# Attention on one core: bias tables loaded in quarters between transposing DMAs, and half of each head's share added by VectorE out of PSUM

## The reference

```python
qkv = (x @ qkv_w.T).reshape(Bb, Ss, 3, H, D)
...
scores = jnp.einsum('bhqd,bhkd->bhqk', q, k) * SCALE
...
dist = jnp.abs(pos[None, :] - pos[:, None])
kb = -p * jnp.log1p(a * dist)
attn = jax.nn.softmax(scores + kb[None], axis=-1)
out = jnp.einsum('bhqk,bhkd->bhqd', attn, v)
...
return out @ out_w.T
```

## Time and profile before

| | us |
|---|---|
| runs, median (lowest, highest) | 1968.41 (1962.46, 1969.35) |
| the profiled execution | 1962.84 |
| its span in the profile | 1961.1 |
| PE busy | 1809.5 |
| DVE busy | 1496.1 |
| ACT busy | 1163.7 |
| POOL busy | 1472.4 |

### The profile page before, as it was taken

One profiled execution on the slowest core, in us unless ns is written; L12 is line 12 of the kernel. 1 busy time (PEld: TensorE's weight loads), 2 busy tenths in 40 slices (PEclk: granted clock), 3 DMA queues, 4 the chain that ended last, 5 costly groups with the idle time before them and its releaser, 6 DMA issues. The chain is left out here.

```text
span 1961.1 us, 39818 instructions
## 1 busy us (share of the span) xinstructions
PE 1809.5 (92%) x12356; PEld 1048.2 (53%) x12356; DVE 1496.1 (76%) x2828; ACT 1163.7 (59%) x1724; POOL 1472.4 (75%) x871
## 2 busy tenths in 40 slices
PE   4999899998699999999999999999999999599988
PEld 3655633333355555555555555555555555256656
DVE  5244589999688788788788788788888788698841
ACT  6553422222677777777677777677777777322133
POOL 5250067778699899899899899899899899555421
PEclk8999999999799999999999999999999999799989
DMA  4254335464598988888888888888888988500001
GB/s 153 90 190 152 84 114 165 155 212 169 137 179 176 197 183 177 194 183 178 193 183 173 188 185 178 190 183 176 194 184 181 200 184 176 123 0 1 1 6 38
DMA packets 714150, 295.28 MB, mean 151 GB/s; under 512 B 619264, under 2 KB 678658, under 8 KB 714064
## 3 DMA queue, kind: packets, MB, share of 16 engines
q1 hardware_dynamic: 674784, 245.23, 56.8%
q10 hardware_dynamic: 37248, 46.14, 6.7%
q0 software_dynamic: 2048, 3.15, 0.6%
HBM read 102.39 MB, written 58.85 MB: 82 GB/s over the span
## 5 line engine op out<-in xcount | busy, mean ns | idle before, releaser
L1223 POOL TENSOR_TENSOR probs_lo<-probs 128x1024 bf16<-128x1024 f32 x512 | 958.1, 1900 | 80.4 <-DMA probs_t_lo<-probs_lo 54.4
L1191 ACT ACTIVATE probs<-scores,neg_max 128x1024 f32<-128x1024 f32 x512 | 588.7, 1150 | 266.2 <-DVE neg_max L1117 231.6
L1117 DVE CUSTOM_DVE_ANT_0 scores<-score_ps,bias_tab 128x1024 f32<-128x1024 f32 x512 | 624.9, 1221 | 120.1 <-issue 113.9
L1040 PE MATMUL score_ps<-k_hi_hi,q_hi_lo 128*128 128x512 bf16 x1024 | 392.8, 384 | 24.6 <-DVE ident_bf L1177 18.1
L1041 PE MATMUL score_ps<-k_lo_lo,q_hi_lo 128*128 128x512 bf16 x1024 | 391.1, 382 | 0.0
L1049 PEld LDWEIGHTS turn_ps<-ident_bf,probs 128*128 128x128 bf16 x4096 | 273.4, 99 | 146.7 <-issue 26.8
L1049 PE MATMUL turn_ps<-ident_bf,probs 128*128 128x128 bf16 x4096 | 316.0, 221 | 20.7 <-ACT probs L1191 20.7
L1068 PE MATMUL pv_ps<-probs_t_hi,v_hi_lo 128*128 128x512 bf16 x1024 | 262.9, 380 | 11.0 <-DVE share L1157 7.6
L1198 ACT COPY probs_t_hi<-turn_ps 128x1024 bf16<-128x1024 bf16 x256 | 255.8, 999 | 20.0 <-PE turn_ps L1049 16.1
L887 PE MATMUL proj_ps<-xn_t,wqk 128*128 128x512 f32 x512 | 232.7, 608 | 7.9 <-DVE rotated L777 5.9
L791 POOL TENSOR_TENSOR qk_parts<-rotated,qk_parts 128x1024 bf16<-128x1024 f32 x64 | 135.9, 2125 | 125.0 <-ACT qk_parts L785 124.7
(11 more groups left out here) (225 smaller groups left out, 2378.4 us busy)
## 6 DMA issues: line engine op xcount, KB each, us to landing
qk_parts<-qk_parts ACTq DMA_DIRECT2D x64, 512.0 KB, 3.4
q_hi_lo<-qk_parts SPq DMA_DIRECT2D x128, 128.0 KB, 2.8
k_hi_hi<-qk_parts SPq DMA_DIRECT2D x128, 128.0 KB, 2.9
k_lo_lo<-qk_parts SPq DMA_DIRECT2D x128, 128.0 KB, 2.9
v_hi_lo<-v_parts SPq DMA_DIRECT2D x64, 256.0 KB, 3.2
bias_tab<-bias_by_distance SPq DMA_DIRECT2D x16, 960.0 KB, 6.6
probs_t_lo<-probs_lo SPq DMA_TRANSPOSE x512, 3.3
v_parts<-cos_tables ACTq DMA_DIRECT2D x12, 512.0 KB, 2.7
```

The costliest lines, as they stand in the source:

```text
L1040: pe.matmul(o[:, cs[c]], QS[s][:, q], KS[s][:, cs[c]], start=True, stop=False)
L1117: v.tensor_tensor_reduce(SB[n % 2][:], sp_[n % 2][:], TB[s][:, j:j + S], -1.0, 3.0e38, ALU.add, ALU.min, neg_max[:, n % 16:n % 16 + 1]).th ...
L1191: act.activation(PR[n % NP][:], SB[n % 2][:], ACT.Exp, bias=neg_max[:, m:m + 1], scale=-1.0, accum_out=row_sum[:, m:m + 1]).then_inc(exped, 1)
L1223: g.tensor_tensor(LQ[n % NL][:], PR[n % NP][:], PRB[n % NP], ALU.subtract).then_inc(low_made, 1)
```

## The change

- `load_table` loads a quarter of a table (480 of 1920 columns, 240 KB).
- In `units`, the quarters of table s = 0 are issued behind `lo_turn` 9 to 12 of the group's last iteration; those of s = 1 behind `lo_turn` 0 to 3 of the next group's first iteration, so behind SP's branch back. A v load at n = 2 or 10 goes ahead of the quarter.
- `bias_max` waits on tile 0 for all four quarters.
- `scale_share` multiplies bank 0 as before. For bank 1 DVE runs four `scalar_tensor_tensor`, one for each row of `K.SACC`: PSUM times the row's scalar, plus the row. `SH` is one buffer, and POOL adds bank 0 alone, once a head.

```diff
@@ project, sync @@
-                load_table(sp, K, 0, s)
+                for k in range(4):
+                    load_table(sp, K, 0, s, k)
...
-def load_table(sp, K, g, s):
-
-    tab = bass.AP(tensor=K.fscr.tensor, offset=(g * 2 + s) * FLEN, ap=[[1, P], [1, TAB]])
-    sp.dma_start(K.TB[s][:], tab).then_inc(K.tab_in[s], DMA)
+def load_table(sp, K, g, s, k):
+
+    n = TAB // 4
+    tab = bass.AP(tensor=K.fscr.tensor, offset=(g * 2 + s) * FLEN + k * n, ap=[[1, P], [1, n]])
+    sp.dma_start(K.TB[s][:, k * n:k * n + n], tab).then_inc(K.tab_in[s], DMA)
...
-    SH = [sb(f"share{i}", [P, 4, D]) for i in range(2)]
+    SH = sb("share", [P, 4, D])
...
+        LOADS = (BT, U - 1)
...
-                    if n in (BT, U - 1) and not (last and b == B - 1):
-                        s = n // (U - 1)
+                    if n in LOADS and not (last and b == B - 1):
+                        s = LOADS.index(n)
...
                         load_scores_in(sp, K, it + 1, s)
-                        if b == B - 1:
-                            load_table(sp, K, g + 1, s)
+                    if LOADS[0] < n <= LOADS[0] + 4 and b == B - 1 and not last:
+                        load_table(sp, K, g + 1, 0, n - LOADS[0] - 1)
+                    k = (n - LOADS[1] - 1) % U
+                    if k < 4 and n > LOADS[1] and b == B - 1 and not last:
+                        load_table(sp, K, g + 1, 1, k)
+                    elif k < 4 and n < BT and b == 0 and not (isinstance(it, int) and it == 0):
+                        load_table(sp, K, g, 1, k)
...
-                    v.wait_ge(tab_in[s], (it + n // U) // B * DMA + DMA)
+                    v.wait_ge(tab_in[s], (it + n // U) // B * (4 * DMA) + 4 * DMA)
...
-                for c in range(2):
-                    v.wait_ge(op_ready, at(it, 4, 2 * hh + c + 1))
-                    v.wait_ge(added, at(it, 4, 2 * hh + c + 1))
-                    v.tensor_tensor(SH[c][:], ov[c][:], last_axis(inv[:, BT * h + 4 * c:BT * h + 4 * c + 4], D),
-                                    ALU.mult).then_inc(scaled, 1)
+                v.wait_ge(op_ready, at(it, 4, 2 * hh + 1))
+                v.wait_ge(added, at(it, 2, hh + 1))
+                v.tensor_tensor(SH[:], ov[0][:], last_axis(inv[:, BT * h:BT * h + 4], D), ALU.mult).then_inc(scaled, 1)
+                v.wait_ge(op_ready, at(it, 4, 2 * hh + 2))
+                v.wait_ge(scaled, at(it, 4, 2 * hh + 2))
+                for k in range(4):
+                    row = (it % B) * BT + 4 + k
+                    acc = K.SACC[:, row, :] if isinstance(row, int) else K.SACC[:, bass.ds(row, 1), :].rearrange("p o d -> p (o d)")
+                    ins = v.scalar_tensor_tensor(out=acc, in0=ov[1][:, k, :], scalar=inv[:, BT * h + 4 + k:BT * h + 5 + k],
+                                                 in1=acc, op0=ALU.mult, op1=ALU.add)
+                ins.then_inc(scaled, 1)
...
-            def add_share(it, h, c):
-
-                g.wait_ge(scaled, at(it, 4, 2 * h + c + 3))
+            def add_share(it, h):
+
+                g.wait_ge(scaled, at(it, 4, 2 * h + 3))
                 g.sem_inc(add_begun, 1)
-                row = (it % B) * BT + 4 * c
+                row = (it % B) * BT
                 acc = K.SACC[:, row:row + 4, :] if isinstance(row, int) else K.SACC[:, bass.ds(row, 4), :]
-                g.tensor_tensor(acc, acc, SH[c][:], ALU.add).then_inc(added, 1)
+                g.tensor_tensor(acc, acc, SH[:], ALU.add).then_inc(added, 1)
...
-                for c in range(2):
-                    if there(u) and u % BT == BT - 2 + c:
-                        add_share(it, u // BT, c)
+                if there(u) and u % BT == BT - 2:
+                    add_share(it, u // BT)
...
-            g.nop().then_inc(added, 2)
+            g.nop().then_inc(added, 1)
```

## The result

| | before | after |
|---|---|---|
| median of four runs each, us (lowest, highest) | 1966.3 (1962.5, 1969.4) | 1993.9 (1991.3, 2000.6) |
| the profiled execution, us | 1962.8 | 2000.6 |
| its span | 1961.1 | 1998.6 |
| head 1 to head 61, us | 1100.4 | 1127.9 |

After over before is 1.0146, 95% interval 1.0112 to 1.0181: slower by 28 us. The forecast was 1994, slower.

The account below looks back on a forecast made before the run. PE was taken to bound the stage at 17.80 us a head. Boundary losses of 61.8 instead of 32.4 us, less 1.2 at the end, gave +28.2; forecast 1994 us, own range 1974 to 2018, 1962 to 2018 with the second rival.

Parts of the forecast that it names:

- What bounds the stage: Attention stage: PE sets the pace at 17.80 us a head; 32.4 us are lost at changes of head pair.
- The share costs 0: VectorE's four adds for one product: +0.44 us a head, covered before PE's scores; taken as 0, bounds 0 and 28 us.
- The rival of adds that block on POOL: VectorE's four adds each wait out a POOL instruction of 1.89 us: +426 us, about 2390; chance 0.04.
- The first table 4.4 us late: Tile 0 at a change of head pair: VectorE waits for the last piece, landed 795.9 against a start at 791.53.
- The walk through SP's queue: Slot-by-slot issue times at one boundary: transpose 1.45 us, copy 0.6; last pieces issued at 792.7 and 815.1, landing 3.2 later.
- The second table 9.2 us late at five boundaries: Tile 0 behind the loop's branch: last piece lands at 818.3 against 809.06, first 4.4 contained; branch gap kept at 5.26 us.
- the second rival: SP's gap at the branch was the table's traffic, 0.3 us in its place: +4.2 us, 1967 to 1973; chance 0.11.
- 4.4 us at the other two: Boundaries entering and leaving SP's loop: no branch gap, second table lands within the first delay, so 4.4 us each.
- The clock, 1.0 a boundary: PE's clock slows after its new idles: cost between 0 and 3.4 us, taken as 1.0 a boundary, 7.0 in all.
- The end of the stage, -1.2 us: Behind the last product POOL adds once, not twice, and VectorE's four adds run beside it: -1.2 us.
- The sum: Whole kernel: +29.4 us at boundaries less 1.2 at the stage's end, +28.2 us; 1991.0 profiled, 1996.6 median.

Follow-up runs that it names:

- e5: The changed kernel with quarters issued earlier (behind transposes 5 to 8 and 13 to 15) and SP's loop over the middle groups written out; ratio 0.9849 to the kernel before.
- e2: The kernel before, tables whole, with only the new share (four adds on VectorE, one on POOL); 1961.7 us against 1967.9 before.
- e11: The kernel before with only the new share, tables whole, run again on another chip; 1960.6 us, ratio 0.9987.
- e4: The changed kernel with the quarters issued earlier, behind transposes 5 to 8 and 13 to 15, ahead of loads and branch; 1943.5 us, ratio 0.9875.
- e6: The changed kernel with quarters issued earlier (behind transposes 5 to 8 and 13 to 15) and the old share; ratio 0.9910 to the kernel before.
- e9: The kernel before with the new share and whole tables issued earlier, behind transposes 5 and 13; 1939.7 us, ratio 0.9870.
- e10: The changed kernel with whole tables, issued where its last quarters were, behind transpose 12 and transpose 3 of the next iteration; ratio 1.0120 to the kernel before.
- e3: The changed kernel with SP's loop over groups 1 to 6 written out, so no branch back; 1977.7 us, ratio 1.0051 to the kernel before.
- e1: The changed kernel with the old share (two products on VectorE, two adds on POOL), tables in quarters; 1996.5 us against 1967.9 before.
- e8: The changed kernel with all four quarters issued one behind the other at the kernel before's place; ratio 1.0023 to the kernel before.
- e12: The changed kernel with all four quarters together at the kernel before's place, run again on another chip; 1967.9 us, ratio 1.0009.

## Why the prediction was right

The sign, the place and the size were right: +28.2 us were summed, 27.6 us came (medians). That the two agree to within 1 us is partly luck: two terms were off by about 5 us each, against each other. The steps one by one:

**What bounds the stage.** PE at 17.80 us a head, with all that can be gained in 32.4 us at the boundaries: shown by e5, which has 1068.2 us for the 60 heads.

**The share costs 0.** It costs nothing, and helps POOL a little. The four adds take 1.12 us together, and the next `bias_max` starts 0.4 us later than behind two products, as forecast; in VectorE's timeline after:

```profile
883.37 0.69 DVE L1165 TENSOR_TENSOR share<-pv_ps,inv_sum 128x512 f32<-128x512 f32 x1
883.97 1.12 DVE L1171 SCALAR_TENSOR_TENSOR s<-pv_ps,inv_sum,s 128x128 f32 x4
885.02 1.22 DVE L1126 CUSTOM_DVE_ANT_0 scores<-score_ps,bias_tab 128x1024 f32<-128x1024 f32 x1
```

From product to `bias_max` that is 1.65 us, where the earlier trace rows has 1.21. What the step left out is that POOL, lighter by 1.3 us a head, has more lead at a stop: the heads take 2 us less in e2 and e11, and 5 less in e4 than in e6. The rival of adds that block on POOL is out: over the whole run an add took 340 to 351 ns.

**The first table 4.4 us late.** Measured against the undisturbed 12.87 us it was 5.1 on average (4.6 to 5.6). The walk through SP's queue holds nearly to the slot. Shifted by 5.21 us (where POOL's `low` stands in the two traces) it puts transpose 9 at 789.7, piece 0 at 791.2 and piece 1 at 793.8; the trace has 789.67, 791.14 and 793.81. The last piece is 0.9 us behind the walk, all of it in the slow issue of piece 1. The landing was mis-sized: 3.8 us, not 3.2.

**The second table 9.2 us late at five boundaries.** Measured the same way (undisturbed 30.41) it was 9.2 on average, 8.5 to 9.5. Two errors cancel here. The gap at the branch, kept at 5.26 us, fell to about 3.3; against it stand the 0.9 us of the first table, the 0.6 of the landing and slots that were a little longer. So the second rival was right in a part: of the gap of 5.26 us about 2 came with the 960 KB queued right ahead. (With the same share, SP is silent for 4.6 to 5.7 us behind the branch in e2 and e11, and for 2.7 to 3.1 in e9 and e10, where the whole table stands elsewhere. By what way the load holds the queue up no run shows.) The other 3 are gone with the loop written out (e3). The Trainium skill (Runtime: NRT & Kernel Launch, section Instruction fetch mechanics) says that a taken branch out of the pages held waits for a fetch; by that rule, the trace of e3 agrees with its 0.72 us against 3.90, though that these 3 us are the fetch itself no run shows.

**4.4 us at the other two.** They lost 6.4 and 6.9. The first wait is 4.8 and 5.3 of that; the rest is a second wait for the table that the walk had landing in time: VectorE idles another 2.2 us at the first of them and 2.1 at the last, put down to "issue" as at the first table, and tile 0 starts 0.15 us behind the table's landing. So two waits came to 13.7 us where 8.8 were forecast: this term was too small by 4.9.

**The clock, 1.0 a boundary.** At each of the seven boundaries PE's granted clock is 0.50 for 3.4 us about its idle at the first table, and it costs nothing in the end: the slow stretch lies between the two waits, and the second ends with a table's landing, whatever PE did before. Behind the second wait a slow stretch follows at two boundaries, the third and the sixth (from 978.58 and 1432.56 us), and there VectorE falls back by another 0.9 and 0.6 us. So of the 7.0 us about 1.5 came, and 5.5 were wrongly added. The window of the slow stretch at the second boundary, with the columns us, busy of PE, PEld, DVE, ACT, POOL, then PEclk, DMA share and GB/s:

```profile
804.50:807.90 3.40, 3.14 (x26) 2.51 (x25) 3.40 (x8) 1.82 (x3) 1.90 (x1) 0.50 0.70 185
```

**The end of the stage, -1.2 us.** In POOL's timeline after, the last add:

```profile
1717.43 1.26 POOL L1246 TENSOR_TENSOR s<-s,share 128x512 f32<-128x512 f32 x1 [7.45 <-DVE share L1165]
```

It ends 3.05 us behind the last head's first output projection (1715.64); in the kernel before the two adds end 4.28 us behind it. The step held.

**The sum.** Forecast as lost were 51.0 us at the five boundaries of the loop and 10.8 at the two others, 61.8 with the clock in; measured were 46.3 and 13.3, 59.6 by boundary. So the terms were off by -4.7 and +2.5, and the sum by 2. The sum's own scale was the profiled execution, 1991.0 there, and that came at 2000.6: of the 37.5 us between the two spans, head 1 to head 61 explains 27.5 and the start of attention 2.7. The last 7.3 are 8.5 us more behind the attention stage, in code that the change doesn't touch, less the 1.2 saved at its end; e1's and e3's profiles have 2 us or less more there. It is one execution and its cause stays open. The median held: 1966.3, by the four runs, and 28.2 are 1994.5. The 1994 itself was a value chosen between 1991.0 and 1996.6.

**Not tried:** a `bias_max` that waits for the one quarter its tile reads, the only use for pieces that would be left.

## What to carry over

In this kernel a load in a hand-ordered queue was priced by the slot of its last part and by what stood behind it, more than by its size: walk the queue slot by slot to the issue of the last piece, add its landing, and compare it with the first reader. The reader here waits for all the pieces, and splitting by itself brought nothing, in the old place or early. Moving the whole table two or three transposes earlier, to where its old contents have just been read and away from the other loads, gave 1.2% (e9 against e11), nearly what the change lost. Where two waits follow on each other, a loss between them is covered by the second, so their costs aren't summed. And where the profile puts a wait for several things down to an engine, compare it with the landing of the load as well.

## What the runs showed of the hardware

- SP's silence behind a taken branch back was 2.6 to 3.5 us where six loads of 128 KB were the last thing queued ahead (after, e1, e4, e6, e9, e10), 3.7 to 5.3 with four quarters as well (e8, e12), 4.6 to 5.7 with a whole table as well (before, e2, e11). With the loop written out (e3), the next transpose was issued 0.7 us behind the start of the sixth load's issue.
- A table of 960 KB landed in 6.4 to 6.8 us (median) behind the six loads, and in 5.6 to 5.7 us apart from them; a quarter of it in 3.8 to 4.2 us, more than the 3.2 of a v load of 256 KB.
- In e5, from 551 to 1672 us, PE had no idle above 0.2 us and its granted clock stayed at 1.00, 2.4 GHz. In the changed kernel it fell to 0.50, 1.2 GHz, for 3.4 us about PE's idle of 3.3 to 4.4 us at the first table of each of the seven boundaries, and twice more behind the second, where PE had idled 3.0 and 3.4 us; after second idles of 2.1 to 2.5 us it didn't. In the kernel before it did once behind an idle of 1.99 us (from 669.0 us), so the length of the idle alone doesn't tell.
- A `scalar_tensor_tensor` of 128x128 with one input in PSUM, one in SBUF and its scalar in SBUF took 340 to 351 ns in all 256 cases of the changed kernel, beside a GpSimd that was busy for 989 of the 1140 us from 550 to 1690 us.
